# Second pass of a fused two-layer kernel: the stores of prepared weights move behind the next unit's kept weights in SyncE's queue

## The reference

```python
x = x + 0.5 * L0_ffn(layernorm(x))    # silu(x W1') * (x W3'), Walsh-Hadamard over 2048, times W2'
x = x + L0_attn(layernorm(x))         # layer norm with gamma, beta; causal softmax; own residual
x = x + 0.5 * L0_ffn(layernorm(x))
x = x + 0.5 * L1_ffn(layernorm(x))    # ternary gate, up, down (1408 wide) with row scales
x = x + L1_mix(layernorm(x))          # tanh(x B') C' + D * x
x = x + 0.5 * L1_ffn(layernorm(x))
```

## Time and profile before

| what | value |
|---|---|
| median of 3 runs | 1679.14 us (1677.66 to 1679.54) |
| profiled execution | 1682.35 us, of which the span of the trace 1680.6 |
| PE busy | 1669.0 us (99%) |
| VectorE, ScalarE busy | 1193.6 us (71%), 821.1 us (49%) |
| DMA | 380.20 MB, mean 226 GB/s |
| granted TensorE clock | 1.00 |

### The profile page before, as it was taken

One profiled execution on the slowest core, in us unless ns is written; L12 is line 12 of the kernel. 1 busy time (PEld: TensorE's weight loads), 2 busy tenths in 40 slices (PEclk: granted clock), 3 DMA queues, 4 the chain that ended last, 5 costly groups with the idle time before them and its releaser, 6 DMA issues.

```text
span 1680.6 us, 21442 instructions
## 1 busy us (share of the span) xinstructions
PE 1669.0 (99%) x7453; PEld 1375.8 (82%) x7453; DVE 1193.6 (71%) x1861; ACT 821.1 (49%) x1307; POOL 124.7 (7%) x185
## 2 busy tenths in 40 slices
PE   9999999999999999999999999999999999999998
PEld 7788888888888888888888888888888888888887
DVE  8888778677777676755446655447778869877866
ACT  5745444456566464433223333223556556655644
POOL 1000000000012220000000000000000143100001
PEclk9999999999999999999999999999999999999999
DMA  8788865699998456357545457444786763388666
GB/s 315 255 319 300 298 253 214 239 362 360 364 369 268 123 141 140 122 170 225 185 145 189 147 179 234 145 162 147 257 278 209 251 224 113 127 268 269 244 225 214
DMA packets 180109, 380.20 MB, mean 226 GB/s; under 512 B 70689, under 2 KB 106657, under 8 KB 174625
## 3 DMA queue, kind: packets, MB, share of 16 engines
q1 hardware_dynamic: 180000, 378.80, 65.1%
HBM read 279.66 MB, written 99.09 MB: 225 GB/s over the span
## 4 chain that ended last, share of the span: by engine, by line
PE 87%; DMA 4%; DVE 3%; SPq 2%; issue 1%; ACT 1%; POOL 0%; ACTq 0%; DVEq 0%; POOLq 0%
PE psum L653 33%; PE psum L655 28%; PE psum L657 25%; DMA w<-w_kept 3%; PE psum L1079 1%; SPq L831 1%; DMA x<-in_w2a 1%; DMA w_scratch<-stage 1%; SPq L669 1%; DMA x_scratch<-xt_swap 0%; DVE prep L2307 0%; DVE att_lo L2236 0%; DMA p_scratch<-p_swap 0%; DVE p_swap L2748 0%; DVE fw_lo L2230 0%
## 5 line engine op out<-in xcount | busy, mean ns | idle before, releaser
L653 PE MATMUL psum<-xc_hi,w 128*128 128x512 f32 x1544 | 603.4, 391 | 3.5 <-DMA w<-w_kept 2.5
L655 PE MATMUL psum<-xc_lo,w 128*128 128x512 f32 x1544 | 601.0, 389 | 0.0
L657 PE MATMUL psum<-xc_hi,w 128*128 128x512 f32 x928 | 361.2, 389 | 0.0
L653 PEld LDWEIGHTS psum<-xc_hi,w 128*128 128x128 f32 x1544 | 289.8, 188 | 69.4 <-issue 5.0
L655 PEld LDWEIGHTS psum<-xc_lo,w 128*128 128x128 f32 x1544 | 289.9, 188 | 59.3
L653 PE MATMUL psum<-w,hid 128*128 128x512 f32 x864 | 337.2, 390 | 0.0
L657 PE MATMUL psum<-w,hid 128*128 128x512 f32 x864 | 336.4, 389 | 0.0
L2320 DVE TENSOR_TENSOR x<-psum,x 128x512 f32<-128x512 f32 x256 | 173.0, 688 | 145.0 <-PE psum L657 144.6
L655 PE MATMUL psum<-w,hid 128*128 128x512 f32 x544 | 211.7, 389 | 0.0
L1683 ACT ACTIVATE psum<-psum 128x512 f32<-128x512 f32 x108 | 62.9, 582 | 297.4 <-PE psum L657 221.8
L657 PEld LDWEIGHTS psum<-xc_hi,w 128*128 128x128 f32 x928 | 174.2, 188 | 36.4
(11 more groups left out here) (183 smaller groups left out, 1995.2 us busy)
## 6 DMA issues: line engine op xcount, KB each, us to landing
w<-w_kept SPq DMA_DIRECT2D x93, 896.0 KB, 6.9
w<-w_kept SPq DMA_DIRECT2D x132, 512.0 KB, 7.3
w<-w_kept SPq DMA_DIRECT2D x55, 640.0 KB, 4.7
w_kept<-w SPq DMA_DIRECT2D x16, 1792.0 KB, 7.6
w<-w_kept SPq DMA_DIRECT2D x93, 256.0 KB, 4.6
w_kept<-prep SPq DMA_DIRECT2D x12, 1792.0 KB, 7.9
w_kept<-w SPq DMA_DIRECT2D x16, 512.0 KB, 7.1
turn_scratch<-swap SPq DMA_DIRECT2D x48, 128.0 KB, 2.5
```

The lines of the kernel that those rows point to most:

```text
L653: pe.matmul(out, a_hi, b_hi, start=start, stop=False, skip_group_check=onto)
L655: last = pe.matmul(out, a_hi, b_lo, start=False, stop=stop and zero == "a", skip_group_check=onto)
L657: last = pe.matmul(out, a_lo, b_hi, start=False, stop=stop, skip_group_check=onto)
```

## The change

`w13_out` and `w2_out` are each cut in two: the wait with the next raw load, and the store (`w13_store`, `w2_store`). For the units of layer A, made in the first pass, the store stays where it was. For the units prepared in the second pass the store is called one slot later, from the slot loop, after that slot's `w13_load` and `w2_load`: the stores of the unit prepared in slot s - 1 are issued in slot s, for s from 2 to 13, and block 28 in slot 13. All waits of all engines stay.

```diff
                 elif W13_BASE["B"] <= n < W13_BASE["S"]:
                     flat_load(n + 1)
+                if n < W13_BASE["B"]:
+                    w13_store(n)
+
+            def w13_store(n):
                 source = w13[:, n % 2, :, :] if n < W13_BASE["B"] else prep13[:, :, :]
                 sp.dma_start(w13_kept[n], source.rearrange("p a n -> p (a n)").bitcast(F32)).then_inc(kept13[n % 2], 16)
@@
                 if n + 2 <= LAST_W2:
                     w2_raw_load(n + 2)
+                if n < W2_BASE["B"]:
+                    w2_store(n)
+
+            def w2_store(n):
                 source = w2[:, n % 4, :, :] if n < W2_BASE["B"] else (prep2_last if n == LAST_W2 else prep2)[:, :, :]
                 sp.dma_start(w2_kept[n], source.rearrange("p a n -> p (a n)").bitcast(F32)).then_inc(kept2[n % 4], 16)
@@
                     if ps.no == 1:
+                        if 2 <= s <= UNITS["B"] + 2:
+                            w13_store(W13_BASE["B"] + s - 2)
+                            w2_store(W2_BASE["B"] + s - 2)
+                            if s == UNITS["B"] + 2:
+                                w2_store(LAST_W2)
                         if s == 0:
                             sp.dma_start(half_down_s[:, :], t["down_s"]).then_inc(hds_in, 16)
                         if 1 <= s <= UNITS["B"] + 1:
                             w13_out(W13_BASE["B"] + s - 1)
```

## The result

The changed kernel took 1752.23 us (median of 5 runs, 1751.26 to 1754.5) against 1679.14 us before. The ratio is 1.0439, with a 95% interval of 1.0427 to 1.0451: 73 us slower. The forecast was +54 us, 1733, in a range up to 1747. The sign, the place and the mechanism came out, the size did not: it was 73 us. The profiled execution took 1754.5 us, the longest of the five.

A forecast was written before the change was run, and what follows sets the result against it. PE was taken as the bound, with DMA nearly full and 2.5 us of weight waits to gain. Eleven late slots, +49.3 us, and +4.5 behind them gave +53.8: 1733 us, own range 1714 to 1747, overall 1712 to 1747.

The forecast's parts named there:

- the place: Second pass: slots 2 to 12 wait, so slot 13 starts 49.3 us later; slots 13 to 15 add the rest.
- the mechanism: Slots 2 to 12: late store holds prep13, closing a loop over ScalarE, VectorE, SyncE and DMA, 19.6 us against PE's 15.0.
- What bounds the kernel: Slots 1 to 13, second pass: PE nearly full, 15.13 us per slot, 14.95 without waits; DMA engines 95% busy.
- the prize: PE's four waits for kept weights, 2.5 us in all, are the most that earlier loads can give back.
- the DMA rate: Sign that the forecast is right: DMA near 285 GB/s in the looping slots.
- the store's time from issue to landing: Sign that the forecast is right: the 1792 KB store lands 11 to 13 us behind its issue.
- Served beside the loads: Rival: SyncE's order does not order landings; store lands at F + 9.3 (F: first raw block's issue), 1676.6 us; 4 in 100.
- The change does nothing: Rival: SyncE reaches the stores at the same time in either order, 1679 us; 1 in 100.
- The clock falls: Rival: PE drops to 1.2 GHz behind idle time, costing slots 12 to 15 1.4 to 4 us, 1736; 5 in 100.
- the 12.1 us for 4352 KB: Slots 2 to 12: time from the second raw block's landing to the 1792 KB store's, mean of five old cycles.
- +4.5: Behind slot 13's start: last three stores delay xt_store(0), stretching slot 14 and delaying slot 15's weights; +4.5 us (0 to 8).
- the queue would be empty when a cycle begins: In the 19.6 us loop the queue is empty when the first raw block is issued, so lateness does not pile up.

The follow-up runs named there:

- the thin load: Changed kernel, loading 112 KB instead of 896 KB of the kept low half for slots 3 to 13 of the second pass: 1730.09 us; on the kernel before: 1677.89 us.

## Why the prediction was right and where it was wrong

**What bounds the kernel, and the prize.** Right. PE was bound by its own work but for 2.5 us; weights that always come in time gave 2.0 us.

**The mechanism.** Right, and shown. The store behind 2304 KB keeps prep13 busy, ScalarE stalls eleven times (68.9 us; 65 to 75 forecast), PE waits in front of p4 for seed_w. The run with the stores in front, the thin load and the two runs with extra DMAs change the place or the bytes, and the loop follows. Of the signs named for it, the DMA rate (261 GB/s, not 285) and the store's time from issue to landing (12.4 to 14.4 us, not 11 to 13) missed on the slow side.

**The rivals.** *Served beside the loads*: fell, the large store takes 14.1 us from issue to landing in its new place. *The change does nothing*: fell. *The clock falls*: it did behind the waits, and the run that kept it up was 2 us faster, inside the 1.4 to 4 us that the rival had for it, though not clear of noise.

**The wrong step** is one term of the sum, the 12.1 us for 4352 KB, "I take the mean". It measured 13.8. Entering eleven times, it makes the first start 1.8 us later, counted from the first raw block (17.6 instead of 15.8), and the ten loops 1.5 us longer (21.12 instead of 19.6): +17 us. Two small terms add to it. Slot 12 runs p4 at the lower clock (6 x 0.2 us), and slots 13 to 15 came to +6.6 instead of +4.5, with the first eight matmuls of slot 13 at the lower clock among them. Together 20.3 us. The trace's span went from 1680.6 to 1752.7, and the changed kernel came to its first cycle 1.95 us earlier (322.30 against 324.25, behind stretches that are the same in both; its second trace had 324.06, so that is chance), so the whole stretch cost 74.1 us in this trace where the sum had 53.8.

Why was the term too small? The 12.1 us were read from cycles in which the large store stands right behind the raw blocks, and there the queue moves 386 GB/s from 2 to 10 us behind the first raw block. In the new order weight loads stand in that place and it moves 307, which is 1.5 us of the 1.7. That the time goes there is shown by the traces; why the rate is lower stays open. It is not the clock, nor a queue that only lacked another load there, nor loads that are slow as such.

The text also said that the queue would be empty when a cycle begins, and then averaged over five cycles of which four began with older transfers under way. The one that began empty, the first (6 GB/s in its first microsecond), took 13.0 us and would have given +64. But all eleven cycles of before took 10.9 to 13.1 us, 12.0 on the mean, and the slowest of them, from 430.53, began with 279 GB/s still flowing. So beginning empty explains some half of the miss at most, and that part is argued, not shown by a run.

A single rate does not describe these 4352 KB: the whole 4352 KB went at 323 GB/s (4.456 million bytes in 13.8 us), while 512 KB more right in front of the store cost 0.9 to 1.2 us and 784 KB less gave 2.0, by the medians 400 to 430 GB/s. Two slips in the text moved little: the slices at 360 to 369 GB/s are the ninth to the twelfth, and 2304 KB at its pace are 6.4 us, not 6.3.

The Trainium skill (DMA: Bandwidth & Descriptors, Bandwidth) gives 425 GB/s for a 16 MB stream. The extra 512 KB (430 by the medians) agree with it, the full 4352 KB (323) do not, and the measurement decides: by the page's figure the forecast would have been lower still.

**The range.** It ended at the slowest of the five cycles read, 13.0. The measured mean of 13.8 lies beyond it, because a cycle in the new order is not one of the old cycles reordered. The upper end needed a margin for that: a loop of 21 us gives 1748 with the forecast's +4.5, and 1752 with the small terms as measured.

## What to carry to other kernels

A store from a single buffer is half of a wait: before it is moved back in a queue, count the bytes that then land in front of it and the slack of whoever refills the buffer; here 2.5 us of waiting for loads were traded for a closed loop over three engines and the DMA queue, 6 us longer than the slot. If work must be issued in one queue, the transfer whose landing closes the loop with the least slack goes first. To let its ready half leave early costs the others nothing; here it gained 1.7 us at most, at the edge of noise. When a change reorders a queue, do not carry over the time of the old order as if bytes alone made it: the same bytes took 12.1 us in one order and 13.8 in the other. Widen the range if no cycle of the old trace has the new order.

## What the runs showed of the hardware that was not expected

- 24 filler matmuls in each of eleven slots brought the granted clock from 0.90 back to 1.00 in that stretch and left the loop as long as it was (20.93 us against 20.94 and 21.12): a lower clock costs little where PE waits anyway.
- Right in front of the large store, 512 KB cost the same whether they were loaded or stored: 1.2 us by the medians, 0.9 by the landings in the traces.
- With the same bytes in another order, the queue moved 307 GB/s instead of 386 from 2 to 10 us behind the first raw block, in each of eleven cycles (287 to 318 against 360 to 396), and the same 1792 KB of weights took 6.4 us instead of 4.8. Another load issued in front of them left the rate at 311, a store there gave 346; the cause is not shown.
